# Output stage of a gated cross-attention kernel: the high-attention by low-context products in 64-row halves, with six output banks

## What is computed

```python
x = x + tanh(g_xattn[0]) * attended            # attended = softmax(scores) @ ctx, ctx: (4, 64, 2048)
h = layernorm(x)
aux_out = (w @ selected_values) @ Wvd.T @ Wvu.T  # Wvu: (2048, 128)
x = x + tanh(g_ffn[0]) * (h + gate[..., None] * aux_out)
```

## Time and profile before

| | |
|---|---|
| median of 3 runs | 1164.13 us (1161.33 to 1164.6) |
| the profiled execution, its own time | 1167.04 us |
| its span, first to last instruction | 1165.2 us |
| granted TensorE clock, mean over the span | 0.96 |
| TensorE busy | 1076.9 us (92%) |
| VectorE busy | 771.4 us (66%) |
| ScalarE busy | 559.5 us (48%) |
| bytes moved | 218.89 MB, mean 188 GB/s |

### The profile page before, as it was taken

The page is one execution under the profiler, slowest core; times in us unless marked ns, Lnnn a source line. Parts: engine busy times, 40 slices in busy tenths (PEclk is TensorE's granted clock), DMA queues, the critical chain, the costliest instruction groups (busy, mean ns, idle before and its releaser), DMA issues. The chain is left out here.

```text
span 1165.2 us, 19595 instructions
## 1 busy us (share of the span) xinstructions
PE 1076.9 (92%) x6890; PEld 1026.1 (88%) x6890; DVE 771.4 (66%) x1820; ACT 559.5 (48%) x868; POOL 180.5 (15%) x337
## 2 busy tenths in 40 slices
PE   6999879878698799999999999999999994899998
PEld 6999879877598799999999999999999994677876
DVE  6555465345512677777777777778777765688776
ACT  4333457636811455454555545455554544455453
POOL 0000060000000131322223132222323221000000
PEclk9999989988889799999999999999999996899999
DMA  7333446665543899364534554354643427699997
GB/s 277 125 140 144 153 173 245 219 236 191 196 75 85 198 245 220 109 175 129 144 87 129 152 153 117 99 144 125 180 105 111 122 95 241 248 364 417 420 427 300
DMA packets 101980, 218.89 MB, mean 188 GB/s; under 512 B 47540, under 2 KB 63956, under 8 KB 82904
## 3 DMA queue, kind: packets, MB, share of 16 engines
q1 hardware_dynamic: 96760, 180.68, 50.4%
q10 hardware_dynamic: 4608, 33.56, 6.9%
q0 software_dynamic: 576, 4.19, 0.9%
HBM read 174.10 MB, written 54.79 MB: 196 GB/s over the span
## 5 line engine op out<-in xcount | busy, mean ns | idle before, releaser
L55 PE MATMUL tk_hidden_sum<-b_weights,k_turned 128*128 128x384 f32 x512 | 176.6, 345 | 0.0
L56 PE MATMUL tk_hidden_sum<-b_weights,k_turned 128*128 128x384 f32 x512 | 173.6, 339 | 0.0
L57 PE MATMUL tk_hidden_sum<-b_weights,k_turned 128*128 128x384 f32 x512 | 173.4, 339 | 0.0
L55 PE MATMUL tk_b_sum<-b_weights,k_turned 128*128 128x320 f32 (+1 forms) x528 | 169.3, 321 | 2.1 <-DVE k_turned L1203 1.6
L57 PE MATMUL tk_b_sum<-b_weights,k_turned 128*128 128x320 f32 (+1 forms) x528 | 163.7, 310 | 0.0
L56 PE MATMUL tk_b_sum<-b_weights,k_turned 128*128 128x320 f32 (+1 forms) x528 | 163.4, 309 | 0.0
L1194 DVE STREAM_TRANSPOSE tk_bank<-k_rows 128x512 f32<-128x512 f32 x128 | 133.9, 1070 | 15.4 <-DMA k_rows<-in_x_dram 15.1
L1013 ACT ACTIVATE k_turned<-tk_bank 128x512 fp32r<-128x512 f32 x128 | 73.9, 595 | 102.6 <-DVE tk_bank L1194 85.4
L55 PEld LDWEIGHTS tk_b_sum<-b_weights,k_turned 128*128 128x128 f32 x528 | 99.3, 188 | 3.2 <-issue 3.0
L56 PEld LDWEIGHTS tk_b_sum<-b_weights,k_turned 128*128 128x128 f32 x528 | 99.4, 188 | 0.0
L55 PEld LDWEIGHTS tk_hidden_sum<-b_weights,k_turned 128*128 128x128 f32 x512 | 97.2, 190 | 2.4
(11 more groups left out here) (270 smaller groups left out, 2592.8 us busy)
## 6 DMA issues: line engine op xcount, KB each, us to landing
k_rows<-in_x_dram SPq DMA_DIRECT2D x48, 1024.0 KB, 4.9
k_rows<-in_x_dram SPq DMA_DIRECT2D x128, 256.0 KB, 5.2
k_rows<-in_Wk_dram SPq DMA_DIRECT2D x16, 1024.0 KB, 4.7
k_rows<-in_Wq_dram SPq DMA_DIRECT2D x16, 1024.0 KB, 4.8
late_x<-in_x_dram SPq DMA_DIRECT2D x16, 1024.0 KB, 14.8
out_dram<-k_rows ACTq DMA_DIRECT2D x16, 1024.0 KB, 9.9
out_dram<-late_x ACTq DMA_DIRECT2D x16, 1024.0 KB, 10.4
b_weights<-scratch_b SPq DMA_DIRECT2D x6, 1024.0 KB, 7.7
```

What stands on the lines that cost most here:

```text
L55: pe.matmul(out, lh, rh, start=start, stop=False, skip_group_check=skip)
L56: pe.matmul(out, lh, rl, start=False, stop=False, skip_group_check=skip)
L57: return pe.matmul(out, ll, rh, start=False, stop=stop, skip_group_check=skip)
```

## The change

Three things change in the output block, and nothing elsewhere.

First, the second matmul of a quarter, [high; low] by ctx2 over 128 rows, becomes high by ctx2 over 64 rows. The product low by low is thereby dropped. Two such matmuls stand in a row: for quarter 2h it reads partitions 0 to 63 of both operands, for quarter 2h + 1 partitions 64 to 127, and they write two different banks. They come first in each half tile (`pair`), before the two times four matmuls over 128 rows that follow.

Second, since both halves of `azT` must now hold the high part, the stack [high; low] gets a buffer of its own, `stack[u]`. ScalarE writes its upper half with one more instruction (64 x 128) ahead of the old copy. VectorE writes its lower half with the instruction that used to write into `azT`.

Third, `po` has six banks in place of four, as three pairs. Half tile q takes pair q mod 3 and waits until the adds of half tile q - 3 are done.

```diff
-        po = [m.ps(f"out{n}") for n in range(4)]
+        stack = [keep["Z"][u][:, 3 * P:4 * P] for u in range(2)]
+        po = [[m.ps(f"out{q}{k}") for k in range(2)] for q in range(3)]
...
-            def chunk(t, u, n, b):
-                if t > 0:
-                    pe.wait_ge(S["added"], 4 * t + n - 3)
-                cols = slice(n * QN, (n + 1) * QN)
-                pe.matmul(po[n][:], azT[u][:, 0:P], ctx1[:, b % 2, cols], start=True, stop=False)
-                pe.matmul(po[n][:], azT[u][:, 0:P], ctx2[:, b % 2, cols], start=False, stop=False)
-                split_product(pe, po[n][:], (azT[u][:, P:2 * P], zl[u]), (wvu[0][:, cols], wvu[1][:, cols]),
-                              False, True).then_inc(S["summed"], 1)
+            def pair(t, u, h, b):
+                q = 2 * t + h
+                if q >= 3:
+                    pe.wait_ge(S["added"], 2 * q - 4)
+                out = po[q % 3]
+                cols = [slice((2 * h + k) * QN, (2 * h + k + 1) * QN) for k in range(2)]
+                for k in range(2):
+
+                    half = slice(k * NCTX, (k + 1) * NCTX)
+                    pe.matmul(out[k][:], azT[u][half, 0:P], ctx2[half, b % 2, cols[k]], start=True, stop=False)
+                for k in range(2):
+                    pe.matmul(out[k][:], stack[u], ctx1[:, b % 2, cols[k]], start=False, stop=False)
+                    split_product(pe, out[k][:], (azT[u][:, P:2 * P], zl[u]),
+                                  (wvu[0][:, cols[k]], wvu[1][:, cols[k]]), False, True).then_inc(S["summed"], 1)
...
-                for n in range(4):
-                    chunk(t, u, n, b)
-                    if n == 1 and t + 1 < TILES:
+                for h in range(2):
+                    pair(t, u, h, b)
+                    if h == 0 and t + 1 < TILES:
                         turn(t + 1, 1 - u)
...
                 act.wait_ge(S["turned"], t + 1)
+                act.activation(stack[u][0:NCTX, :], turn_ps[u][0:NCTX, 0:P], ACT.Copy)
                 act.activation(azT[u], turn_ps[u][:, 0:2 * P], ACT.Copy).then_inc(S["hi"], 1)
...
-                dve.tensor_tensor(azT[u][NCTX:P, 0:P], turn_ps[u][NCTX:P, 0:P], f32(azT[u][NCTX:P, 0:P]),
+                dve.tensor_tensor(stack[u][NCTX:P, :], turn_ps[u][NCTX:P, 0:P], f32(azT[u][NCTX:P, 0:P]),
                                   ALU.subtract)
...
-                dve.tensor_tensor(x[s][:, cols], x[s][:, cols], po[n][:], ALU.add).then_inc(S["added"], 1)
+                dve.tensor_tensor(x[s][:, cols], x[s][:, cols], po[(2 * t + n // 2) % 3][n % 2][:],
+                                  ALU.add).then_inc(S["added"], 1)
```

## The result

| | median | runs | beside the kernel before |
|---|---|---|---|
| before | 1164.13 us | 1159.82 to 1164.86, 5 runs | |
| changed | 1172.31 us | 1171.36 to 1176.85, 5 runs | ratio 1.0091, 95% interval 1.007 to 1.0112 |

The change makes the kernel slower by 8.2 us by the two medians, where +6.2 had been forecast. The ratio in the table is higher than that of the two medians (1.0070), and would be 10.6 us. The kernel before has medians of 1162.5 to 1163.2 us in the later groups of runs, against which the changed kernel stands 9.1 to 9.8 us higher. So its price is known to about 2 us only. The profiled execution of the changed kernel has a span of 1175.0 us against 1165.2.

A forecast was written before the change was run, and what follows sets the result against it. TensorE was taken as the output block's limit, with DMA equal within 2%. Terms +7.8 (pairs), +0.3 (copy), -0.4 (scaling waits) and -1.5 (last context) gave +6.2 us, 1170.3 us; range 1158.5 to 1180 us.

The forecast's parts named there:

- The direction and its cause: Output block: slower, as 64-row matmuls overlap but switching costs more than that saves, TensorE being the limit; +6.2 us.
- The excursion: TensorE, each half tile: going from 128-row matmuls to 64-row ones and back costs about 0.30 us (0.27 to 0.33) beyond streaming.
- the pair: The two 64-row matmuls of a half tile: 0.59 us against 0.467 before, between 0.50 and 0.67; 64 of them, +7.8 us.
- The second weight load: The pair's second matmul has its own weight load: 0.11 us if it holds back, 0 if hidden, taken as 0.055.
- The wait of 1.5 us at the last context: TensorE's wait for the last context's transfers: goes, since a later TensorE finds it landed; -1.5 us.
- The three waits for the scaling: TensorE's waits for the next tile's scaling on VectorE: remain, each shorter by 0.12 us; -0.4 us.
- The copy: Extra 64 x 128 copy on ScalarE: 0.26 us, hidden except at the first tile; +0.3 us.
- Six banks: Output banks: no effect expected, since TensorE never waited for the adds.
- No overlap: Rival: the two 64-row matmuls run one after another, a pair costs 0.77 us; +17.1 us, 1181 us; chance 0.13.
- The fast rival: Cheap switches and full overlap, a pair 0.24 to 0.35 us; transfers limit the gain to about -5 us, 1159 us; chance 0.21.
- the slack of the last x load: Last tile's x load lands 2.6 us before its use; counted as limiting what a faster TensorE could gain.
- idle DMA time: DMA engines at the output block's start: some 4 us left idle, of which 2 to 3 us counted as usable.

The follow-up runs named there:

- e1: The changed kernel with both 64-row matmuls of a half tile reading partitions 0 to 63: 1186.25 us (one run).
- e3: The changed kernel with its order, banks and copy, but the two low-context matmuls over 128 rows as before: 1162.77 us, ratio 0.9998 to the kernel before.
- e6: The changed kernel with the two 64-row matmuls of a half tile apart, one in each of 128 excursions: 1209.19 us (one run).
- e8: The changed kernel with the two 64-row matmuls in the plain f32 form: 1211.88 us (one run).
- e5: The changed kernel with four output banks in place of six: 1172.51 us, ratio 1.0086 to the kernel before.
- e4: The changed kernel without its 64-row matmuls, the product of high attention and low context left out: 1152.85 us, ratio 0.9916 to the kernel before.
- e12: The same kernel as e7, run on the same chip as e11: 1163.16 us, ratio 1.0003 to the kernel before.
- e2: The changed kernel with all four 64-row matmuls of a tile together at its start, one excursion a tile: 1160.77 us, ratio 0.9973 to the kernel before.
- e7: e2 with the low part of the next context cut into four pieces on VectorE: 1162.96 us, ratio 1.0004 to the kernel before.
- e11: The same kernel as e2, on another chip: 1161.40 us, ratio 0.9982 to the kernel before.

## Why the prediction was right

**The direction and its cause** held, step by step: overlap, a price for the excursion above what the overlap saves, TensorE as the limit. e1, e3 and e6 show each apart.

**The excursion** was the term of the sum that was mis-sized: 0.27 to 0.33 us, taken as 0.30, measured 0.39. e8 rules out the form. What the rows had was less than the whole. The price has four parts, two for each change: 0.09 us ahead of the pair, 0.11 behind its first matmul (e1), 0.09 ahead of L1493 and 0.11 behind it. In the earlier trace rows they read 0.09 + 0.12 + 0.06 = 0.27, with a matmul of 48 columns in the middle. The full reading of the earlier trace rows is 0.09 + (0.53 - 0.427) + (0.52 - 0.427) + 0.06 = 0.34; the prediction had these as 0.29 and 0.06, and its upper end of 0.33 is their sum made slightly too small. So the rows of before fall short of the measured price by 0.05, and that lies in the last part, 0.06 there and 0.11 here. The matmul behind was a transpose there, whose weight load takes 0.14 us, and is a product here, whose load takes 0.19. That this difference makes the 0.05 was not tried.

**The second weight load**, taken as 0.055 between 0 and 0.11, costs 0, by e6. The two errors are of opposite sign, 0.09 too little and 0.055 too much, and that they nearly cancel is luck: the pair was to cost 0.59 and costs 0.62, inside the 0.50 to 0.67 given.

**The smaller terms.** The wait of 1.5 us at the last context went. The three waits for the scaling shrank by 0.6 us (0.4 said). The copy costs 0.27 us and shows only at the first tile, by 0.15 us (0.3 said). Six banks do nothing, by e5. With the measured pair the sum is 64 x 0.153 + 0.15 - 0.6 - 1.5 = +7.9 us. With the 1.1 us of the lower clock at the start of the block it is 9.0, against 8.7 in the profiled block. The sum of the prediction had no term for that clock, whose share differs from one execution to the next.

**The rivals.** "No overlap" had for it that the two L607 follow each other at full length. They are two records of one matmul (e8), so the row was no evidence for it at all. The fast rival's limit was of the right kind and too tight by 5 us. I took the slack of the last x load, 2.6 us, and 2 to 3 us of idle DMA time for the whole; in e4 the block takes 1151.1 - 991.44 = 159.7 us, 11.1 less than before. The rows of e4 show 409 GB/s from 1010 to 1050 us, where the kernel before has 364 in the same stretch (share 0.96) and the changed one 351, so more of the start of the block was usable than I counted. That this is the whole of the 5 us is argued, not shown.

## What to carry to other kernels

Running two matmuls over 64 rows at the same time works, but each trip from 128-row matmuls into them and back costs 0.39 us, more than one 512-column matmul of 0.234 that it saves. By these numbers it pays only where a trip carries two or more pairs (0.39 + 2 x 0.234 = 0.86 us for what takes 0.93 over 128 rows), so gather them before tuning anything else. Even then the gain here was 0.2 to 0.3%, at the edge of what the runs can tell. Before making an engine faster, take its work out altogether once (as in e4): 10 us of 30 said at once that the next thing to look at was the order of the transfers. And when a wait of TensorE grows, read its clock behind the wait as well: in e12 3.8 us of waiting cost 6.4.

## What was not expected of the hardware

Each change between 128-row and 64-row matmuls costs 0.20 us, 0.09 ahead of the first matmul of the new kind and 0.11 behind it. So the price of an excursion is the same for one matmul, a pair or four (e2: from L57 at 1010.63 to L55 at 1011.96 it is 1.33 us, less 4 x 0.234 = 0.39), and the same in both forms (0.39 and 0.40 us). Matmuls over 66 rows don't pay it. Two weight loads of 128 columns into the two halves take 0.18 us together. Even with both in one half, as in e1, the second load adds nothing: from the pair to L1493 it is 0.66 us, the 0.43 of a single matmul and 0.23 more to stream the second.

TensorE's granted clock fell to 0.50 during waits of 2.9 us (e7), 3.8 us (e12) and 10.0 us (e4) and stayed there for some us of full work. After the waits of 1.4 to 2.1 us (e11, before, e2) it was 1.00.
